# Two post-norm transformer layers on one core: attention outputs turned on VectorE, first batch projected in place, and a new deal of the steps

## The chip, the cores and the metric

One NeuronCore of a Trainium2 chip runs the whole program. The metric is the device time of one execution in microseconds (us), median over the runs shown. Everything is fp32.

## What is computed

The input x is 8 batches of 256 tokens with 128 features. Two layers follow, each an attention and a feed-forward part, each with a residual and a layer norm behind it:

```
x = layernorm(x + attn0(x))     # 16 heads of 8, softmax over 256 keys, biases
x = layernorm(x + ffn0(x))      # 128 -> 512, butterfly mixes, GELU, butterfly mixes, 512 -> 128
x = layernorm(x + attn1(x))     # low-rank q and kv, RoPE, causal, 16 heads on 4 kv heads
x = layernorm(x + ffn1(x))      # h = silu(gate) * up, hidden 384
```

The butterfly stages of ffn0 are folded on the chip into two dense matrices (`wup`, `down`) during the first steps.

## The kernel before

**Batches and steps.** The 8 batches of layer 0 are batches 0 to 7, those of layer 1 are 8 to 15, so there are 16 batches of 16 heads, 256 heads in all. Each engine has one program, and all five walk the same list of steps `STEPS` (L49), two heads a step. The step number g is the head whose exponentials are due. In a step TensorE issues the row-maximum scores of heads g+14 and g+15 (`max_scores`, L292, banks SM) and the scores to be exponentiated of heads g and g+1 (`exp_scores`, L311, banks ST), and behind them whatever is due at this g. There are three SM banks and three ST banks, so a score matmul waits until VectorE (the maximum, L668 in layer 0, L676 in layer 1) or ScalarE (the exponential, L535) has read the head three before. All other TensorE results share two G banks, handed out in order by `claim`, which waits for the last reader of the bank.

**What is due when** is an order written out by hand, the constants `AT_...` (L43 to L48): an item of batch b is due at g = 16b + offset, one of a feed-forward tile n of layer 0 (512 tokens, two batches) at 32n + offset. "Slot s" below means steps with g mod 16 = s; slots of the 32-step cycle of a tile of layer 0 are given mod 32. Per batch: projection of queries and keys (`AT_QK`, L447), values (`AT_V`, L461), two transposes of maxima (`AT_MT`, L348), products with the values for each half of the heads (`AT_PV`, L479), then the tail of the attention: ScalarE copies each half out (O, L597); at `AT_T` TensorE transposes four 128x128 blocks (L355), VectorE takes reciprocals of the row sums and multiplies (L684, L687); at `AT_ATT` TensorE transposes two blocks back (L405) and ScalarE copies (L555); at `AT_PROJ` the output projection (L415) follows; then statistics on VectorE, the norm on GpSimd (`AT_LN`, L780), transposes (L422). Layer 0 adds four up matmuls (L365), one GELU over 2048 columns on ScalarE (L602, with a table load ahead and one behind), two down groups (L389), norm and transposes. Layer 1 adds RoPE on GpSimd (`AT_ROPE`, L832 to L834), the causal mask on GpSimd (L824), three up matmuls (L376), a down group (L398).

**Queries and keys** leave the projection with one feature row per partition and are laid out by DMAs (L231, four a batch) into `QK`, where head j of a group has 32 rows of its own; row 31 of each strip takes the negated maximum (sent by a DMA from `mt`, L246) against a row of ones. `QK` has a ring of four batches.

**Start.** Batch 0 goes the same way: load, projection, copy, four DMAs. Before the first scores TensorE runs three 128x512 matmuls on a zeroed part of `QK` (L453), which GpSimd clears first (L815). Steps -14 to -2 fill the ST side with dummy matmuls (`filler`, L322). Weights for later stages are loaded by SP, one DMA a step from g = LATE = -20 on (L249).

Of the kernel before, what the change touches and what calls it, by code (L numbers as in the profile page):

```python
# [38 lines left out]
VCOL, VPAD = 32, 264  # L39
# [12 lines left out]
FIRST, FINAL = AT_QK, HEADS + 40  # L52
STEPS = range(FIRST, FINAL, 2)


def batch_at(g, offset, layers=(0, 1)):

    b, rest = divmod(g - offset, H)
    return b if rest == 0 and 0 <= b < BATCHES and b // NB in layers else None

# [14 lines left out]
def block_kernel(nc, x_nat, x_t, ones, wqk0, wv0, bqk0, bv0, wproj, bproj, u0, d0, fac_u, fac_d, bfw, bup, bcon, bdown,  # L75
# [7 lines left out]
    with ctx:  # L83
# [3 lines left out]
        def sem(name):  # L87
            return ctx.enter_context(nc.semaphore(name))

        wqk_sb = sb("wqk_sb", [P, 2, W])  # L90
# [47 lines left out]
        O = sb("O", [P, 2, 2, T])  # L138
        rec = sb("rec", [P, 4 * QT * 2, 2])
        at = sb("at", [P, QT, W])  # L140
# [15 lines left out]
        ld = {n: sem(f"ld_{n}") for n in ("x0", "x", "qk", "v", "id", "bf", "up", "bv", "bvc", "xb", "proj", "l1", "next", "rope", "gate")}  # L156
# [3 lines left out]
        bv_ps, filled = sem("bv_ps"), sem("filled")  # L160
        path_ready = [sem(f"path_ready{i}") for i in range(2)]
# [8 lines left out]
            "st_ps", "exp_done", "masked", "pv_ps", "o_ready", "t_ps", "at_ready", "att_ps", "att_ready", "proj_ps",  # L170
# [27 lines left out]
        def _(sp):  # L198
            sp.dma_start(xt[:, 0:T], x_t[:, 0:T]).then_inc(ld["x0"], 16)
            sp.dma_start(id32[:, :], ident).then_inc(ld["id"], 16)  # L200
            sp.dma_start(xt[:, T:TOK], x_t[:, T:TOK]).then_inc(ld["x"], 16)
            sp.dma_start(wv_sb[:, :], wv0).then_inc(ld["v"], 16)

            late = [(ld["bv"], wproj_sb[:, :], wproj), (ld["bv"], bproj_sb[:, :], over_partitions(bproj)),
                    (ld["up"], facs[0][:, :, :], fac_u), (ld["up"], u_sb[:, :, :], u0),
                    (ld["xb"], xb[:, :, :], x_nat),
                    (ld["bf"], bfw_sb[:, :, :, :, :], bfw), (ld["bf"], d_sb[:, :, :], d0),
                    (ld["bf"], facs[1][:, :, :], fac_d), (ld["bf"], bup_sb[:, :], bup)]
# [8 lines left out]
            for g in STEPS:  # L217
                for l in range(2):
                    if (b := batch_at(g, AT_QKIN[l], (l,))) is not None:

                        if l == 0:
                            sp.wait_ge(A["qk_out"], 2 * (b + 1))
                        else:
                            sp.wait_ge(A["rotated"], b - NB + 1)
                        if b < QK_RING:
                            sp.wait_ge(zeros_ready, b + 1)
                        else:
                            sp.wait_ge(A["st_ps"], H * (b - QK_RING + 1))

                        for j in range(2 if b == 0 else STRIPS):  # L230
                            sp.dma_start(QK[STRIP * j:STRIP * j + ROWS, b % QK_RING, :, :, :], qk[j:P:STRIPS, b % 2, :, :])\  # L231
                                .then_inc(qk_in[b % QK_RING], 16)
                        if b < QK_RING:
                            sp.dma_start(QK[MAXROW:P:STRIP, b, :, 1, :], ones).then_inc(ones_in[b], 16)
                if (b := batch_at(g - 2, AT_QK, (1,))) is not None:
# [7 lines left out]
                if (n := half_at(g - 2, AT_MT)) is not None:  # L243
                    b, t = divmod(n, 2)
                    sp.wait_ge(A["mt_ready"], n + 1)
                    sp.dma_start(QK[MAXROW:P:STRIP, b % QK_RING, 2 * t:2 * t + 2, 0, :], mt[:, n % 2, :]).then_inc(m_in[n % 4], 16)  # L246
# [11 lines left out]
        def _(pe):  # L258
# [19 lines left out]
            def max_scores(m, c):  # L278

                b, r, j = place(m)  # L280
                if c == 1:
                    if m % H == 0:
                        pe.wait_ge(qk_in[b % QK_RING], 16 * STRIPS * (b // QK_RING + 1))
                    if m >= S_RING:
                        pe.wait_ge(A["max_done"], m - S_RING + 1)
# [10 lines left out]
            def exp_scores(m, c):  # L296

                b, r, j = place(m)
                if c == 0:
# [3 lines left out]
                    if m % H == 0 and b < QK_RING:  # L303
# [3 lines left out]
                    else:  # L307
                        pe.wait_ge(filled, m + LEAD - S_RING + 1)
# [7 lines left out]
            def filler(m, c):  # L316
# [3 lines left out]
                if c == 0 and m >= S_RING - LEAD:  # L320
                    pe.wait_ge(filled, m + LEAD - S_RING + 1)
# [5 lines left out]
            def scores(g):  # L327

                for long in range(2):
# [3 lines left out]
                    for m in (g, g + 1):  # L333
                        if 0 <= m < HEADS:
                            exp_scores(m, long)
                        elif -LEAD <= m < 0:
                            filler(m, long)

            for g in STEPS:
                scores(g)  # L340

# [8 lines left out]
                if (b := batch_at(g, AT_T)) is not None:  # L350
                    bank = claim(("t", b), A["at_ready"], b + 1, g)
                    pe.wait_ge(A["o_ready"], 2 * (b + 1))
                    for q in range(QT):
# [3 lines left out]
                    ins.then_inc(A["t_ps"], 1)  # L357
# [43 lines left out]
                if (b := batch_at(g, AT_ATT)) is not None:  # L401
                    bank = claim(("att", b), A["att_ready"], b + 1, g)
                    pe.wait_ge(A["at_ready"], b + 1)
                    for q in range(QT):
                        ins = nc.tensor.transpose(bank[:, q * P:(q + 1) * P], at[:, q, :], id32[:, :])  # L405
                    ins.then_inc(A["att_ps"], 1)
# [23 lines left out]
                if (b := batch_at(g, AT_QK)) is not None:  # L430
                    x = xt[:, (b % NB) * T:(b % NB + 1) * T]
                    if layer(b) == 0:
                        bank = claim(("qk", b), A["qk_out"], 2 * (b + 1))
                        if b == 0:
                            pe.wait_ge(ld["x0"], 16)
                            pe.wait_ge(ld["qk"], 32)
                        elif b == 1:
                            pe.wait_ge(ld["x"], 16)
# [10 lines left out]
                if g == FIRST:  # L449

                    pe.wait_ge(zeros_ready, QK_RING)
                    for i in range(3):
                        nc.tensor.matmul(ST[i][:, :], QK[:, QK_RING - 1, 0, 0, 0:P],  # L453
# [555 lines left out]
```

## Time and profile before

| | |
|---|---|
| median of 3 runs | 377.0 us (376.42, 377.0, 378.9) |
| the profiled execution, its own time | 378.37 us |
| its span, first to last instruction | 376.6 us |
| around the span | 1.8 us |
| TensorE matmul busy | 341.9 us (91%) |
| VectorE busy | 238.1 us (63%) |
| ScalarE busy | 203.9 us (54%) |
| GpSimd busy | 170.8 us (45%) |
| mean granted TensorE clock | 0.970 |

Busy shares are means over stages; the span has a start (to 28 us), a layer 0 part (to about 190 us), a layer 1 part, and a tail without scores from about 355 us on. An fp32 matmul shows as two records in the profile, so "x4" is two matmuls.

### The profile page before, as it was taken

Reading aid. Unit: us, or ns where it says so; the run is one execution under the profiler, and the core shown is the slowest. Engines: PE = TensorE matmul, PEld = TensorE weight load, DVE = VectorE, ACT = ScalarE, POOL = GpSimd, SP = SyncE. Lnnn points to the kernel's source line nnn. Section 1 sums busy time; section 2 is a strip of 40 time slices with the busy share of each in tenths; the row PEclk is TensorE's granted clock in tenths of the full one; section 3 lists DMA queues with packets and bytes.
Section 4 is the critical chain, followed back from the end, with each engine's and each line's share of the span. In section 5 each row is a group of like instructions: output and inputs, shape, how many; then the busy total and the mean of one; then the engine's idle time right before and its main releaser. Section 6 shows DMA issues by size and latency. Waiting matters only on the chain.

```text
span 376.6 us, 10486 instructions
## 1 busy us (share of the span) xinstructions
PE 341.9 (91%) x3912; PEld 239.6 (64%) x3912; DVE 238.1 (63%) x907; ACT 203.9 (54%) x439; POOL 170.8 (45%) x284
## 2 busy tenths in 40 slices
PE   3989999999989999899998899799899999999872
PEld 2557666665648556575567666488677777777652
DVE  3365566577758577376764738548597878883354
ACT  2015666665694656746574545834665565656310
POOL 7036964020202502346143766616958685453621
PEclk9998999999999999899998989969999999999998
DMA  4493150101010101101111001110111111000000
GB/s 146 63 293 58 35 138 3 30 3 30 3 30 2 31 3 31 29 3 30 30 31 28 21 13 30 30 28 4 44 32 44 31 44 30 18 3 17 2 15 29
DMA packets 9219, 14.04 MB, mean 37 GB/s; under 512 B 2001, under 2 KB 4945, under 8 KB 9041
## 3 DMA queue, kind: packets, MB, share of 16 engines
q1 hardware_dynamic: 8656, 13.11, 15.1%
q8 instruction: 31, 0.51, 0.6%
q10 hardware_dynamic: 512, 0.26, 0.4%
q14 instruction: 20, 0.16, 0.2%
HBM read 5.76 MB, written 1.05 MB: 18 GB/s over the span
## 4 chain that ended last, share of the span: by engine, by line
PE 79%; POOL 6%; DVE 5%; ACT 4%; issue 3%; DMA 2%; POOLq 0%; DVEq 0%; ACTq 0%
PE SM L292 27%; PE G L479 13%; PE ST L311 6%; PE G L389 5%; PE G L376 4%; PE G L365 4%; PE G L447 3%; PE G L348 3%; PE G L355 3%; PE G L398 2%; PE G L461 2%; POOL QK L815 2%; PE G L415 2%; DMA QK<-mt 2%; PE ST L453 1%
## 5 line engine op out<-in xcount | busy, mean ns | idle before, releaser
L535 ACT ACTIVATE E<-ST 128x512 f32<-128x512 f32 (+1 forms) x256 | 125.4, 541 | 89.0 <-PE ST L311 88.8
L311 PE MATMUL ST<-QK 32*128 32x256 f32 (+1 forms) x1024 | 138.5, 380 | 9.6 <-ACT E L535 8.0
L292 PE MATMUL SM<-QK 31*128 31x256 f32 (+1 forms) x1024 | 140.2, 379 | 0.8 <-DVE mx L668 0.7
L292 PEld LDWEIGHTS SM<-QK 31*128 31x128 f32 x1024 | 93.3, 186 | 40.5 <-DVE mx L668 13.2
L668 DVE TENSOR_REDUCE mx<-SM 128x2 f32<-128x512 f32 x128 | 82.2, 685 | 56.5 <-PE SM L292 56.3
L311 PEld LDWEIGHTS ST<-QK 32*128 32x128 f32 x1024 | 91.8, 187 | 14.1 <-ACT E L535 9.9
L676 DVE CUSTOM_DVE_ANT_0 masked_s<-SM,mask_sb 128x256 f32<-128x256 f32 (+1 forms) x256 | 75.7, 351 | 36.2 <-PE SM L292 35.9
L824 POOL TENSOR_SCALAR_AFFINE_SELECT E<-E 128x512 f32<-128x512 f32 x64 | 39.1, 634 | 43.5 <-ACT E L535 43.5
L479 PE MATMUL G<-E,V 128*32 128x256 f32 x992 | 53.6, 356 | 0.0
L479 PEld LDWEIGHTS G<-E,V 128*32 128x32 f32 x992 | 28.4, 109 | 20.3 <-issue 4.6
L777 POOL TENSOR_SCALAR nm_a<-mv_a 128x2 f32<-128x2 f32 x15 | 2.9, 193 | 62.7 <-DVE mv_a L635 62.7
L376 PE MATMUL G<-xt,wf 128*128 128x256 f32 x84 | 23.0, 400 | 0.1
L597 ACT ACTIVATE O<-G 128x256 f32<-128x256 f32 x31 | 11.9, 384 | 18.0 <-PE G L479 18.0
L676 DVE DVE_READ_ACCUMULATOR2_ANT mx<- 128x1 f32 x256 | 21.2, 83 | 0.0
L777 POOL TENSOR_SCALAR nm_f<-mv_f 128x4 f32<-128x4 f32 x4 | 0.8, 195 | 43.0 <-DVE mv_f L635 43.0
L389 PEld LDWEIGHTS G<-down,hid 128*128 128x128 f32 x128 | 17.8, 220 | 1.0 <-issue 0.7
L389 PE MATMUL G<-down,hid 128*128 128x128 f32 x128 | 18.3, 303 | 0.0
L376 PEld LDWEIGHTS G<-xt,wf 128*128 128x128 f32 x84 | 15.0, 197 | 3.1 <-ACT mt L542 0.9
L365 PE MATMUL G<-xt,wup 128*128 128x512 f32 x32 | 16.8, 606 | 0.0
L542 ACT ACTIVATE mt<-G 8x256 f32<-8x256 f32 x32 | 11.4, 357 | 7.1 <-PE G L348 7.1
L447 PE MATMUL G<-xt,wqk_sb 128*128 128x256 f32 x32 | 9.9, 434 | 4.7 <-DMA bqk_sb<-bqk 4.7
L832 POOL TENSOR_TENSOR ry<-ry,ropec_sb 128x512 f32<-128x512 f32 x8 | 10.2, 1279 | 8.3 <-issue 4.9
(135 smaller groups left out, 453.8 us busy)
## 6 DMA issues: line engine op xcount, KB each, us to landing
QK<-qk SPq DMA_DIRECT2D x62, 64.0 KB
rs<-ry SPq DMA_DIRECT2D x16, 128.0 KB, 2.3
xb<-x_nat SPq DMA_DIRECT2D x1, 1024.0 KB, 8.1
out<-ln_g SPq DMA_DIRECT2D x8, 128.0 KB, 2.0
xt<-x_t SPq DMA_DIRECT2D x1, 896.0 KB, 6.7
wi<-wi_all SPq DMA_DIRECT2D x1, 576.0 KB, 4.9
QK<-mt SPq DMA_DIRECT2D x32, 8.0 KB
fac<-fac_u SPq DMA_DIRECT2D x1, 508.0 KB, 4.6
```

The lines of the kernel that those rows point to most:

```text
L292: ins = nc.tensor.matmul(SM[m % S_RING][:, cols], q, QK[rows, b % QK_RING, r, 1, keys], start=True, stop=True)
L311: ins = nc.tensor.matmul(ST[m % S_RING][:, c * T:(c + 1) * T - q0], QK[rows, b % QK_RING, r, 1, c * P:(c + 1) * P], QK[rows, b % QK_RING, ...
L365: nc.tensor.matmul(bank[:, :], wup[:, c * P:(c + 1) * P], xt[:, n * FT:(n + 1) * FT], start=True, stop=True).then_inc(F0["up_ps"], 1)
L376: ins = nc.tensor.matmul(bank[:, s * T:(s + 1) * T], wf[:, s, c * P:(c + 1) * P], xt[:, i * T:(i + 1) * T], start=True, stop=True)
L389: ins = nc.tensor.matmul(bank[:, i * W:(i + 1) * W], hid0[:, c, s * P:(s + 1) * P], down[:, c, :], start=(c == 0), stop=(c == HC - 1))
L447: ins = nc.tensor.matmul(bank[:, s * T:(s + 1) * T], w[:, s, :], x, start=True, stop=True)
L479: ins = nc.tensor.matmul(bank[VCOL * j:VCOL * (j + 1), q0:T], values, E[:, (2 * n + e) % E_RING, j, k * T:(k + 1) * T - q0], start=(e == 0 ...
L535: act.activation(E[:, a % E_RING, j, 0:n], ST[m % S_RING][:, 0:n], ACT.Exp, scale=SCALE)\
L597: act.activation(O[:, b % 2, t, :], g_bank["pv", n][:, 0:T], ACT.Copy).then_inc(A["o_ready"], 1)
L668: ins = nc.vector.tensor_reduce(mx[:, n % 2, :, i], bank[:, :].rearrange("p (q k) -> p q k", q=QT), AX.X, ALU.max, negate=True)
L676: ins = nc.vector.tensor_tensor_reduce(out=masked_s[:, m % 2, lo:hi], in0=bank[:, lo:hi], in1=mask_sb[:, T + lo - hi:T], scale=-1.0, scala ...
L824: nc.gpsimd.affine_select(out=e, in_=e, pattern=[[0, 4], [1, P]], compare_op=ALU.is_ge, fill=0.0, base=0, channel_multiplier=-1).then_inc( ...
```

## The change

1. **Attention outputs on VectorE.** The ScalarE copies O and att and both sets of TensorE transposes go. VectorE transposes each PV bank in 32x32 blocks into `turned` (one 128x256 instruction at each PV step), takes reciprocals at `AT_NORM` = 22, GpSimd multiplies (128x256), and at `AT_ATT` = 24 VectorE transposes the product into `att`. The order of the value columns is changed to match.
2. **Batch 0 in place.** `wfirst` holds, for each of the four head groups, the query and key weights already spread over the 32-row strips; four projections (at g = -44, -12, -8, -4) are copied by ScalarE straight into `QK`, with the row of ones as a bias. No layout DMAs for batch 0. The three first matmuls read a tile `idle` that VectorE clears. The filler runs for 8 heads, not 14.
3. **Loads.** Weights of later stages are issued by SP right behind x; only the rest waits for `LATE` = -2. Batch 1's four layout DMAs are issued by ScalarE.
4. **A new deal.** See the constants: odd batches' queries and keys at 16b - 44 (the step behind GELU's), even ones of layer 1 at 16b - 40, values of layer 0 at -8 (even) or -2 (odd), the third up matmul of layer 1 at 44 (was 40), the third of layer 0 at 64 (was 56), RoPE at -34 (was -28), the last norm at 56 (was 50). SP now looks for the DMA of the maxima before the layout DMAs.

```
-AT_QK, AT_QKIN, AT_ROPE = -34, (-32, -24), -28
-AT_MT, AT_V, AT_PV = (-6, 2), 0, (12, 20)
-AT_T, AT_ATT, AT_PROJ, AT_LN, AT_XT = 22, 24, 26, 28, 32
-AT_UP1, AT_DN1, AT_LN1 = (34, 38, 40), 46, 50
-AT_UP0, AT_GELU, AT_DN0, AT_LN0, AT_XT0 = (50, 54, 56, 66), 66, (70, 72), 74, 80
-BXU, BXD, TURN, JOIN, BV, XB_AT, WF_AT, LATE = (4, 6), 16, 32, 22, 0, 14, 38, -20
+AT_QK, AT_QKIN, AT_ROPE = (-34, -40, -44), -28, -34
+AT_MT, AT_V, AT_PV = (-6, 2), ((-8, -2), (0, 0)), (12, 20)
+AT_NORM, AT_ATT, AT_PROJ, AT_LN, AT_XT = 22, 24, 26, 28, 32
+AT_UP1, AT_DN1, AT_LN1 = (34, 38, 44), 46, 56
+AT_UP0, AT_GELU, AT_DN0, AT_LN0, AT_XT0 = (50, 54, 64, 66), 66, (70, 72), 74, 80
+BXU, BXD, TURN, JOIN, BV, XB_AT, WF_AT, LATE = (4, 6), 16, 32, 22, 0, 14, 38, -2
+FIRST, FINAL = AT_QK[2], HEADS + 44
+FIRST_AT, EARLY, FILL = (FIRST, -12, -8, -4), (None, -10, 2), 8
...
# TensorE
+            pe.wait_ge(idle_ready, 1)
+            for i in range(S_RING):
+                nc.tensor.matmul(ST[i][:, :], idle[:, 0:P], idle[:, :], start=True, stop=True)
...
+                for r in range(GROUPS):
+                    if g == FIRST_AT[r]:
+                        bank = claim(("first", r), first_out, 2 * (r + 1))
...
+                        for s in range(2):
+                            ins = nc.tensor.matmul(bank[:, s * T:(s + 1) * T], wfirst_sb[:, r, s, :], xt[:, 0:T], start=True, stop=True)
...
-                        for t in range(2):
-                            ins = nc.tensor.transpose(bank[:, (2 * q + t) * P:(2 * q + t + 1) * P],
-                                                      O[:, b % 2, t, q * P:(q + 1) * P], id32[:, :])
...
-                        ins = nc.tensor.transpose(bank[:, q * P:(q + 1) * P], at[:, q, :], id32[:, :])
...
# ScalarE
-                    act.activation(att[:, :], g_bank["att", b][:, 0:T], ACT.Copy).then_inc(A["att_ready"], 1)
...
-                    act.activation(O[:, b % 2, t, :], g_bank["pv", n][:, 0:T], ACT.Copy).then_inc(A["o_ready"], 1)
...
+                            act.activation(QK[:, 0, r, s, :], g_bank["first", r][:, s * T:(s + 1) * T], ACT.Identity,
+                                           bias=bfirst_sb[:, r, s:s + 1]).then_inc(first_out, 1)
...
# VectorE
+                    nc.vector.reciprocal(rec[:, :, :], found[:, :, 2 * D:2 * D + 2]).then_inc(A["rec_ready"], 1)
...
+                    nc.vector.transpose(att[:, :].rearrange("p (x t c) -> p x t c", t=2, c=2 * D), at[:, :, :, :].rearrange("p t x c -> p x t c"))\
+                        .then_inc(A["att_ready"], 1)
...
+                    nc.vector.transpose(turned[:, t, :], g_bank["pv", n][:, 0:T]).then_inc(A["turned"], 1)
...
# GpSimd
+                    nc.gpsimd.tensor_tensor(at[:, :, :, :].rearrange("p t x (e d) -> p (t x) e d", d=D),
+                                            found[:, :, 0:2 * D].rearrange("p x (e d) -> p x e d", d=D),
+                                            rec[:, :, :].unsqueeze(3).broadcast_to([P, 2 * T // BLOCK, 2, D]), ALU.mult)\
+                        .then_inc(A["at_ready"], 1)
```

## Rows read from the trace of the kernel before

**Rows 1.** Busy time by stage: PE, PEld, DVE, ACT, POOL, clock, DMA.
```profile
87.00:214.00 127.00, 120.28 (x1388) 79.37 (x1390) 83.14 (x268) 78.82 (x153) 40.62 (x68) 0.97 0.10 20
...
286.00:341.00 55.00, 54.09 (x730) 41.76 (x722) 43.76 (x247) 32.92 (x84) 35.30 (x64) 1.00 0.13 28
```

**Rows 2.** Groups by line: the second set of transposes (busy, mean ns, idle before).
```profile
L405 PE MATMUL G<-id,at 128*128 128x128 f32 x30 | 5.8, 275 | 0.2 <-DVE at L687 0.2
```

**Rows 3.** Groups by line on the other engines: busy, mean ns, idle before.
```profile
L687 DVE TENSOR_TENSOR at<-G,rec 128x256 f32<-128x256 f32 x15 | 6.4, 424 | 0.5
...
L697 DVE TENSOR_SCALAR hid<-G,bhid 128x512 f32<-128x512 f32 x16 | 12.0, 747 | 0.4 <-PE G L365 0.3
L597 ACT ACTIVATE O<-G 128x256 f32<-128x256 f32 x31 | 11.9, 384 | 18.0 <-PE G L479 18.0
...
L832 POOL TENSOR_TENSOR ry<-ry,ropec_sb 128x512 f32<-128x512 f32 x8 | 10.2, 1279 | 8.3 <-issue 4.9 <-DMA rs<-ry 3.4
...
L853 POOL TENSOR_TENSOR xb<-ln_a,bcon_sb 128x256 f32<-128x256 f32 x8 | 5.9, 735 | 0.7
```

**Rows 4.** The chain in layer 1, slots 6 to 12: start, us, what.
```profile
289.86 0.41 PE SM L292 x2
...
290.72 0.59 PE G L355 x4
291.31 0.88 PE G L376 x4
...
295.48 0.38 PE G L348 x2
...
296.31 0.41 PE SM L292 x2
```

**Rows 5.** Timeline of VectorE, 288 to 308 us: its idle times.
```profile
290.74 0.42 DVE L676 CUSTOM_DVE_ANT_0 masked_s<-SM,mask_sb 128x256 f32<-128x256 f32 x1 [0.75 <-PE SM L292]
...
299.50 0.42 DVE L676 CUSTOM_DVE_ANT_0 masked_s<-SM,mask_sb 128x256 f32<-128x256 f32 x1 [0.74 <-PE SM L292]
```

**Rows 6.** Timeline of the start, 0 to 31 us.
```profile
7.65 1.88 ACTq L577 DMA_DIRECT2D QK<-qk  x2
...
7.90 5.18 PE L453 MATMUL ST<-QK 128*128 128x512 f32 x6 [1.15 <-POOL QK L815]
...
13.97 0.48 PE L292 MATMUL SM<-QK 31*128 31x256 f32 x2
...
22.36 0.58 SPq L246 DMA_DIRECT2D QK<-mt  x1
...
28.24 0.48 PE L311 MATMUL ST<-QK 32*128 32x256 f32 x2 [1.64 <-DMA QK<-mt]
```

**Rows 7.** Timeline around the first GELU, layer 0.
```profile
101.16 1.13 PE L447 MATMUL G<-xt,wqk_sb 128*128 128x256 f32 x4
...
109.92 1.28 ACT L535 ACT_TABLE_LOAD   x1
...
111.87 0.48 PE L311 MATMUL ST<-QK 32*128 32x256 f32 x1 [1.85 <-ACT E L535]
```

**Rows 8.** The chain behind the first and the third GELU.
```profile
113.58 1.79 PE G L389 x16
...
201.35 1.04 PE G L355 x4
202.40 2.51 PE G L389 x16
...
216.37 0.89 POOL ln_a L780 x2
...
217.40 0.63 PE G L422 x2
```

**Rows 9.** The chain in the tail, 354 to 366 us.
```profile
356.90 0.39 ACT O L597
...
360.63 0.70 PE SM L415 x4
```

More of the change, by code:

```diff
@@ L59, in batch_at, with by_layer, projected_at, values_at @@
     return b if rest == 0 and 0 <= b < BATCHES and b // NB in layers else None
+def by_layer(g, offsets):
+    found = [batch_at(g, offsets[l], (l,)) for l in range(2)]
+    return found[0] if found[0] is not None else found[1]
+def projected_at(g):
+    if g in EARLY:
+        return EARLY.index(g)
+    b = batch_at(g, AT_QK[2])
+    if b is not None and len(EARLY) <= b < BATCHES - 1 and b % 2 == 1:
+        return b
+    b = by_layer(g, AT_QK)
+    return b if b is not None and b >= len(EARLY) and (b % 2 == 0 or b == BATCHES - 1) else None
+def values_at(g):
+    for l in range(2):
+        for parity in range(2):
+            b = batch_at(g, AT_V[l][parity], (l,))
+            if b is not None and b % 2 == parity:
+                return b
+    return None
+def loads_of(b):
+    return b // QK_RING + (1 if b % QK_RING else 0)
 def half_at(g, offsets):
@@ L88, in sem @@
             return ctx.enter_context(nc.semaphore(name))
+        wfirst_sb = sb("wfirst_sb", [P, GROUPS, 2, W])
+        bfirst_sb = sb("bfirst_sb", [P, GROUPS, 2])
+        idle = sb("idle", [P, 512])
         wqk_sb = sb("wqk_sb", [P, 2, W])
@@ L154, in block_kernel @@
         G = [ctx.enter_context(nc.psum_tensor(f"G{i}", [P, 512], F32)) for i in range(2)]
-        ld = {n: sem(f"ld_{n}") for n in ("x0", "x", "qk", "v", "id", "bf", "up", "bv", "bvc", "xb", "proj", "l1", "next", "rope", "gate")}
+        ld = {n: sem(f"ld_{n}") for n in ("x0", "x", "first", "groups", "qk", "v", "id", "bf", "up", "bv", "bvc", "xb", "proj", "l1", "next", "rope", "gate")}
         zeros_ready, v_clean, half_ready = sem("zeros_ready"), sem("v_clean"), sem("half_ready")
@@ L217, in _ @@
             for g in STEPS:
[L218 to L235, printed above, removed]
+                if (n := half_at(g - 2, AT_MT)) is not None:
+                    b, t = divmod(n, 2)
+                    sp.wait_ge(A["mt_ready"], n + 1)
+                    sp.dma_start(QK[MAXROW:P:STRIP, b % QK_RING, 2 * t:2 * t + 2, 0, :], mt[:, n % 2, :]).then_inc(m_in[n % 4], 16)
+                b = projected_at(g - 2)
+                if b is None or layer(b) == 1:
+                    b = batch_at(g, AT_QKIN, (1,))
+                if b is not None and b != 1:
+                    if layer(b) == 0:
+                        sp.wait_ge(A["qk_out"], 2 * b)
+                    else:
+                        sp.wait_ge(A["rotated"], b - NB + 1)
+                    if b < QK_RING:
+                        sp.wait_ge(zeros_ready, b)
+                    else:
+                        sp.wait_ge(A["st_ps"], H * (b - QK_RING + 1))
+                    for j in range(STRIPS):
+                        sp.dma_start(QK[STRIP * j:STRIP * j + ROWS, b % QK_RING, :, :, :], qk[j:P:STRIPS, b % 2, :, :])\
+                            .then_inc(qk_in[b % QK_RING], 16)
+                if (b := projected_at(g - 2)) is not None and layer(b) == 1:
                     sp.wait_ge(A["y_out"], b - NB + 1)
@@ L448, in _ @@
                     ins.then_inc(A["qk_ps"], 1)
[L449 to L453, printed above, removed]
-                                         QK[:, QK_RING - 1, 0, :, :].rearrange("p s t -> p (s t)"), start=True, stop=True)
-                if (b := batch_at(g, AT_V)) is not None:
+                if (b := values_at(g)) is not None:
                     bank = claim(("v", b), A["v_ready"], b + 1)
@@ L813, in _ @@
             nc.gpsimd.memset(half[:, :], -0.5).then_inc(half_ready, 1)
-            for i in range(QK_RING):
+            for i in range(1, QK_RING):
                 nc.gpsimd.memset(QK[:, i, :, :, :], 0.0).then_inc(zeros_ready, 1)
@@ L967, in _arrays @@
     kcol = [2 * D * (h // rep) + 2 * d, 2 * D * (vh // rep) + 2 * vd + 1]
+    wfirst, bfirst = np.zeros((P, GROUPS, 2, P), np.float32), np.zeros((P, GROUPS, 2), np.float32)
+    bfirst[MAXROW::STRIP, :, 1] = 1.0
+    for s, cols in enumerate((q, k)):
+        for i, c in enumerate(cols):
+            row, head = divmod(i, H)
+            to = STRIP * (head % STRIPS) + row
+            wfirst[:, head // STRIPS, s, to], bfirst[to, head // STRIPS, s] = wqkv[:, c], bqkv[c]
     u = np.concatenate([a["L0_ffn_W_exp"].T, a["L0_ffn_b_exp"][:, None]], 1)
```

162 lines of the change are left out of this document (85 added, 77 removed).

## The prediction

> **What bounds the kernel now.** First the busy time by stage [rows 1]: TensorE has 95% of the stretch 87 to 214 us and 98% of 286 to 341 us. So between the ends TensorE's own list of work is the time, and each item taken off it counts unless another wait comes up behind it. VectorE is next: 80% in 286 to 341 us (43.76 of 55.00). Its timeline [rows 5] shows between two idle times, 290.74 and 299.50 us, four steps without a pause. The chain there [rows 4] leaves TensorE after the matmul at 291.31 and comes back only at 295.48, through VectorE. So slots 6 to 10 of a layer 1 batch are already VectorE's, the rest TensorE's. Then the start [rows 6]: the first real scores stand at 13.97 us and the first exponential scores at 28.24 us, where TensorE waits for the DMA of the maxima, issued 22.36 us. Then GELU [rows 7]: ScalarE reloads its table at 109.92, and TensorE stands 1.85 us for an exponential. Last, behind the GELUs [rows 8]: this GELU is the third, and behind it four-block transposes took 1.04 us against 0.59 in rows 4, the sign of a TensorE clock of 1.2 GHz instead of 2.4 after a stall, and the transposes at 217.40 wait for GpSimd's norm (end at 217.26).
>
> **Removed on TensorE.** Per batch 0.59 us of four transposes [rows 4] and about 0.29 of two (5.8 us over 15 batches is 0.38 with overlap, [rows 2]; start to start it is less). 16 x 0.88 = 14.1 us is the most this can give. ScalarE loses three copies of 0.38 a batch [rows 3], which is off the path except in the tail.
>
> **Added.** VectorE gets three 128x256 block transposes a batch and loses one multiply; the reciprocal stays. The trace has no VectorE transpose. Nearest rows [rows 3]: 0.42 us for a 128x256 multiply and 0.75 us for a 128x512 pass. I take 0.42 (same element count, one pass) and keep 0.25 to 0.75 as ends, the lower since part of a short instruction overlaps its neighbour. So VectorE has 3 x 0.42 - 0.42 = +0.84 us a batch, 13.4 us in all. Two of the three stand behind a PV group, the longest item of TensorE, where VectorE idles (the 0.75 us of rows 5), at no cost. The third stands in slot 8, in VectorE's own stretch. GpSimd gets a multiply of 0.74 us [rows 3], between reciprocal (slot 6) and transpose (slot 8); a step lasts 1.6 us or more, so it is hidden.
>
> The Trainium skill (VectorE: DVE Perf Modes, section "The three transpose paths") gives 311 ns for a 128x128 bf16 transpose on VectorE, in 32x32 blocks. If 256 columns cost two of these, an estimate of 0.62 us from that page, the transpose in slot 8 would cost 0.2 more a batch, 3.2 in all, and the time would be 365.6 instead of 362.4. No row here shows a VectorE transpose; it is to be read from the run.
>
> **Slots 6 to 12, the heart.** Layer 1 before: 6.45 us from the start of slot 6 (289.86) to that of slot 12 (296.31) [rows 4]. After: slot 6 loses 0.59, slot 8 loses 0.29 and the third up matmul (0.88), which goes to slot 12. TensorE alone would need 4.7. VectorE's list is two heads (1.1 us a step), reciprocal 0.35, two up passes 0.84, transpose 0.42: slot 8's first maximum is ready 3.8 us after slot 6 starts, so slot 10 can't start before that, and slot 12 starts at 5.35. With 0.88 paid at slot 12 this is 6.2: a gain of 0.25 where slot 8 is else empty. Where it holds the projection (0.87, every second batch) the hole is filled, and the gain is 1.1. That makes 1.4 us in two batches, of 1.8 removed. In layer 0 it is the same with the values (0.6) in slot 24: 0.3 of 0.88 kept there, and 0.4 in the half without up matmuls.
>
> **The sum by stages**, against the profiled execution's own 378.37 us (span 376.6 and 1.8 around it):
> - *Start.* The layout DMAs of batch 0 and the 7 us wait for GpSimd's clears go. Warm-up from about 2 to 7.3 us (5.18, [rows 6]), projection of the first group 1.1 to 2, copy 0.85: scores at about 9.3 instead of 13.97. But then each of groups 1 to 3 is projected in the step just ahead of its first score, so TensorE waits 1.0 + 0.9 us for matmuls and ScalarE's copy, three times, and ScalarE issues batch 1's four DMAs between (1.88 us for two, so 3.3 to 3.8), ahead of group 2's copy: about 3 us of stall. Step 0 comes at about 26 us, as before (25.9). The gain is behind it: the maxima's DMA, 5.8 us then in a queue of big loads, is now issued when these have landed; 2.3 us of wait end. Batch 2's and 3's projections come into steps 2 and 4 where the values left and steps were short. I take 2.5 us; 0 to 5.
> - *Steps 0 to 66*, before the first GELU: transposes in three batches, partly VectorE's: 1.3.
> - *66 to 130*, two tile cycles of layer 0. GELU pins its exponential at 111.87 [rows 7], so the odd batch's projection (1.06 to 1.13 us) behind GELU costs nothing; after the stall 0.59 of transposes goes, but the down group's bank is read by ScalarE's copy of that projection, which ends 0.3 late: 0.3. Further on, norm on GpSimd arrives at the same time as TensorE now, so the lighter slots 8 and 14 there are eaten by that wait. From XT0 to the next GELU 1.1. So 1.4 a cycle, 2.8.
> - *130 to 194.* There GpSimd's chain decides [rows 8]. In the first tile 0.6 off the head of it and 0.4 later: 1.0. In the second the third up matmul is also gone from ahead of the down group, 0.59 + 0.9 + 0.5: 2.0. RoPE (3 x 1.28, [rows 3]) now stands ahead of the mask of heads 12 to 15 instead of behind; PV needs it 5.8 us after XT at the tightest, GpSimd needs 5.1: close, taken as 0.
> - *194 to 256*: 62/32 x 1.4 = 2.7.
> - *Tail.* ScalarE copy, transposes, up matmuls in the way, transposes, copy: from 356.90 to 360.63 is 3.73 us [rows 9]. After: 0.42 + 0.35 + 0.74 + 0.42 and four hand-overs of 0.1 = 2.4. Gain 1.3.
> - *Clock.* Behind three of the four GELUs the clock fell. In rows 8 that cost 0.45 on the transposes (1.04 against 0.59) and 0.7 on the down group (2.51 against 1.79), with scores between 1.5; three times, and the last stall held it twice as long: about 5 in all. With 1.1 us of matmuls in each stall it may not fall; against that stand new stalls in the start. I take 1.0, nearer to nothing, since the wait at XT stays.
> Sum: 2.5 + 1.3 + 2.8 + 3.0 + 2.7 + 1.3 + 1.0 = 14.6. So 363.8 for an execution like the profiled one. That one lay 1.4 above the median, so 377.0 - 14.6 = 362.4 us, a ratio of 0.961. Its own range is 359 to 367.
>
> **Rivals.**
> 1. *The clock stays up.* The silence of TensorE behind GELU shrinks by 1.1 us. For it: the down group behind the stall of rows 7 ran at full clock (1.79, [rows 8]), so not every such stall costs it. Against: the wait at XT behind it remains. All 5.0 instead of 1.0: 358.4.
> 2. *VectorE transposes are dear or its list decides more widely.* At 0.75 us each 1.0 more a batch, of which a third stands in the full stretch and some of the rest at PV: 16 x 0.4 = 6.4 less: 368.8. For it: 80% busy already; against: the rows of equal shape.
> 3. *The start gives nothing or costs.* If TensorE falls to its lower clock without the filler in steps -14 to -10 and in the 3 us stall, its seven steps take 0.5 more each and the gain of 2.5 turns into -1.5: 366.4.
> 4. *Slower than before: GpSimd becomes the pace of layer 1.* In each batch it holds masks 4 x 1.22, RoPE 3.8, norms 4, and now a multiply for which it waits behind VectorE's reciprocal with the next mask queued behind. If PV waits on that mask, each of 8 batches pays multiply, wait and RoPE's rest: 0.74 + 0.6 + 1.1 = 2.4, 19.5 in all, of which the 14.6 pays most: 377.0 - 14.6 + 19.5 = 381.9. It decides once GpSimd is past 17 us in a batch; [rows 1] give it 35.30 of 55.00 us, 64%. So it is unlikely.
> 5. *The change doesn't do what it says*: the removed work was cover for waits throughout, result within 1%: the 95% and 98% of rows 1 speak against it.
>
> **Chances.** Forecast 0.50; clock up 0.18; dear VectorE 0.13; start 0.13; GpSimd 0.03; nothing 0.03. A difference under about 1% can't be told from none here. Faster by over 1% takes the first four: 0.94; same 0.03; slower 0.03. The range takes in the clock rival to most of its size and cases 2 and 3 together: 355 to 370.
>
> **What would show it.** TensorE has no transposes but those of maxima and norms, and its busy sum falls by 12 to 15 us. VectorE shows three transposes a batch, 0.4 us each, busy up by some 13 us, with the waits of max scores on VectorE longer. First real score near 9 us, first exponential score near 26, with a stall for ScalarE's copies between. At GELU the stall on the exponential is about 1 us shorter with a projection ahead of it. Tail from last PV to output projection 2.4 us. Wrong if the VectorE transpose is far from 0.42, if step 0 comes later than 28 us, or if PV waits for the mask over 0.5 us a batch.

## Result: a quarter of the forecast

The changed kernel takes 375.3 us (median of 20 runs, 372.96 to 378.79) beside 378.9 us for the kernel before (20 runs on the same chip). The ratio is 0.991, 95% interval 0.989 to 0.993. The forecast was 0.961, or 14.6 us. The profiled execution of the changed kernel has a span of 373.5 us against 376.6 before, so 3.1 us are there. The direction was right, the size was not.

**Where it came and went.** The step number g names the same point in both kernels, so the start of the first score matmul of a step (timeline of TensorE) can be set side by side. "End" is the end of TensorE's last matmul.

| from the start of | to | before, us | changed, us | gain | forecast |
|---|---|---|---|---|---|
| span | step 8 | 36.94 | 40.72 | -3.8 | +2.5 |
| step 8 | 66 | 67.17 | 65.01 | +2.2 | +1.3 |
| 66 | 130 | 88.69 | 85.09 | +3.6 | +2.8 |
| 130 | 194 | 92.64 | 87.52 | +5.1 | +3.0 |
| 194 | 254 | 65.62 | 65.32 | +0.3 | +2.7 |
| 254 | end | 20.22 | 24.48 | -4.3 | +1.3 |
| clock | | | | in the rows above | +1.0 |
| sum | | | | +3.1 | +14.6 |

So the middle gave more than was forecast (10.9 against 7.1 and the clock's 1.0), the two ends lost 8.1 where 3.8 had been expected, and steady layer 1 gave nothing.

**The profile after.** First the page of the changed kernel: busy time and its share, and two groups, then a third from the list of groups.

```profile
span 373.5 us, 10260 instructions
...
PE 340.0 (91%) x3804; PEld 234.7 (63%) x3804; DVE 250.9 (67%) x940; ACT 189.2 (51%) x397; POOL 178.1 (48%) x299
...
L885 POOL TENSOR_TENSOR at<-turned,rec 128x256 f32<-128x256 f32 x16 | 10.1, 628 | 94.9 <-DVE rec L726 94.9
...
L805 DVE STREAM_TRANSPOSE turned<-G 128x256 f32<-128x256 f32 x31 | 13.9, 449 | 16.8 <-PE G L524 16.6
```
```profile
L731 DVE STREAM_TRANSPOSE att<-at 128x256 f32<-128x256 f32 x16 | 7.0, 437 | 0.0
```

The block transpose on VectorE takes 0.45 us out of PSUM and 0.44 us out of SBUF, beside the 0.42 that was taken from [rows 3]. VectorE's sum rose by 12.8 us, as forecast (13). TensorE's sum fell by only 1.9 us where 12 to 15 were forecast, although the transposes are gone. The granted clock explains little of that: 22.7 us of TensorE's busy time stand at the lower clock, against 19.8 before. Part of the fall was never there to be had: where records overlap the sum counts them once, and without those of L355 and L405 the sum of the kernel before is 11.0 us less, not the prediction's 14.1. Part 1 of the change alone takes 7.0 off it (334.9 us, see the experiments); where the rest went isn't settled. The clock does explain why a later version with the same 10260 instructions shows 330.6: it has only 5.9 us of busy time at the lower clock, 16.8 less, and half of that is 8.4 of the 9.4 us between the two. This is the first thing to learn here: busy time isn't work.

**The start**, against [rows 6]. TensorE, then ScalarE (start us, us, engine, line, what, idle before and its releaser; L406 projects a group of batch 0, L498 queries and keys of batch 1):

```profile
6.39 1.03 PE L406 MATMUL G<-xt,wfirst_sb 128*128 128x256 f32 x4
8.34 1.13 PE L342 MATMUL SM<-QK 31*128 31x256 f32 x10 [0.93 <-ACT QK L610]
...
13.37 2.07 PE L342 MATMUL SM<-QK 31*128 31x256 f32 x8 [0.93 <-ACT QK L610]
15.37 2.08 PE L498 MATMUL G<-xt,wqk_sb 128*128 128x256 f32 x4
...
19.40 1.23 PE L406 MATMUL G<-xt,wfirst_sb 128*128 128x256 f32 x4
...
22.47 0.48 PE L342 MATMUL SM<-QK 31*128 31x256 f32 x2 [1.39 <-ACT QK L610]
...
27.50 0.48 PE L342 MATMUL SM<-QK 31*128 31x256 f32 x2 [0.93 <-ACT QK L610]
```
```profile
18.36 3.17 ACTq L626 DMA_DIRECT2D QK<-qk  x4
21.57 0.84 ACT L610 ACTIVATE QK<-G,bfirst_sb 128x256 f32<-128x256 f32 x2 [3.25 <-PE G L406]
```

The first score stands at 8.34 instead of 13.97, 5.6 us early where 4.7 were forecast. All of it is gone by step -6 (22.47 against 19.91). Each of the three later projections stands just ahead of its first score, and ScalarE's copy is waited for each time; the four DMA issues of L626 hold the second of these copies back (projection ended 20.6, copy begins 21.57); and L498 takes 2.08 us here against 1.06 elsewhere. That last one is the clock. Busy time by stage, of the changed kernel (us, PE, PEld, DVE, ACT, POOL, then the granted clock):

```profile
12.00:20.00 8.00, 7.07 (x33) 4.19 (x32) 2.09 (x4) 1.68 (x4) 7.37 (x13) 0.57 0.07 23
20.00:30.00 10.00, 7.34 (x71) 4.97 (x73) 4.68 (x9) 2.32 (x6) 5.17 (x6) 0.99 0.40 143
30.00:38.00 8.00, 8.00 (x54) 4.99 (x48) 3.45 (x7) 3.58 (x8) 4.51 (x1) 0.58 0.00 1
```

Before, the same stretches had 1.00, 0.99 and 0.80. TensorE is at 1.2 GHz for most of 12 to 20 us and again of 30 to 38.

**Layer 1, slots 6 to 12**, against [rows 4] and [rows 5]: the chain (start, us, what) and VectorE's timeline.

```profile
282.99 0.41 PE SM L342 x2
...
283.86 1.06 PE G L435 x4
...
285.78 1.06 PE G L498 x4
...
288.54 0.41 PE SM L342 x2
...
289.41 1.06 PE G L435 x4
290.47 1.44 PE G L524 x32
```
```profile
283.06 0.45 DVE L805 STREAM_TRANSPOSE turned<-G 128x256 f32<-128x256 f32 x1
283.87 0.42 DVE L716 CUSTOM_DVE_ANT_0 masked_s<-SM,mask_sb 128x256 f32<-128x256 f32 x1 [0.36 <-PE SM L342]
...
284.99 0.35 DVE L726 RECIPROCAL rec<-turned 128x32 f32<-128x32 f32 x1
...
287.27 0.44 DVE L731 STREAM_TRANSPOSE att<-at 128x256 f32<-128x256 f32 x1
```

From slot 6 to slot 12 it is 5.55 us (forecast 5.35), VectorE having no pause in it behind 283.87, and then the third up matmul (289.41) costs 1.06 (forecast 0.88). This is the batch with a projection in slot 8 (285.78); the two behind it, without one, take 5.56, so that projection is hidden, as forecast.

**Behind the third GELU**, against [rows 8], the chain:

```profile
198.96 2.01 PE G L448 x16
...
208.66 1.26 POOL xb L924
...
212.43 0.89 POOL ln_a L834 x2
...
213.45 0.41 PE G L475 x2
```

The first down group takes 2.01 us where [rows 8] have 2.51 behind transposes of 1.04. GpSimd's norm is still what TensorE waits for, at 213.45.

**The tail**, against [rows 9], the chain:

```profile
351.75 0.45 DVE att L731
...
352.33 0.70 PE ST L468 x4
...
355.97 0.34 DVE gated L751
...
356.33 0.43 DVE hid L753
...
356.90 2.31 PE ST L457 x12
359.21 0.44 PE G L475 x2
...
360.20 2.05 PE G L435 x4
362.25 2.86 PE SM L435 x8
```

Before, the output projection (360.63) was followed by norm and transposes alone, and the transposes stood 3.79 us behind it (364.42). Now they stand 6.88 behind (359.21), since VectorE's two passes for the third up of the batch before (355.97) and its down group (356.90) are in between.

### The profile page after: what moved, and what is told of

Read it like the earlier page. It is cut to its first block, busy times and chain, and to the rows that moved or that the text cites. A ratio compares the mean times of both kernels' runs of the same rounds, so it can differ in the third digit from the quotient of the medians.

```text
span 373.5 us, 10260 instructions
## 1 busy us (share of the span) xinstructions
PE 340.0 (91%) x3804; PEld 234.7 (63%) x3804; DVE 250.9 (67%) x940; ACT 189.2 (51%) x397; POOL 178.1 (48%) x299
## 4 chain that ended last, share of the span: by engine, by line
PE 73%; POOL 9%; issue 6%; ACT 5%; DVE 5%; ACTq 1%; POOLq 0%; DVEq 0%
PE SM L342 26%; PE G L524 10%; PE ST L361 6%; PE G L435 5%; PE G L448 4%; PE G L498 4%; PE G L424 3%; PE G L457 2%; PE G L415 2%; PE G L506 2%; POOL ln_f L834 2%; ACT L580 1%; PE G L468 1%; POOL xb L924 1%; PE ST L392 1%
## 5 line engine op out<-in xcount | busy, mean ns | idle before, releaser
L342 PE MATMUL SM<-QK 31*128 31x256 f32 (+1 forms) x1024 | 146.6, 384 | 8.0 <-ACT QK L610 4.2
L342 PEld LDWEIGHTS SM<-QK 31*128 31x128 f32 x1024 | 97.7, 189 | 49.0 <-DVE mx L708 13.3
L885 POOL TENSOR_TENSOR at<-turned,rec 128x256 f32<-128x256 f32 x16 | 10.1, 628 | 94.9 <-DVE rec L726 94.9
L805 DVE STREAM_TRANSPOSE turned<-G 128x256 f32<-128x256 f32 x31 | 13.9, 449 | 16.8 <-PE G L524 16.6
L448 PE MATMUL G<-down,hid 128*128 128x128 f32 x128 | 16.3, 281 | 0.1
L435 PEld LDWEIGHTS G<-xt,wf 128*128 128x128 f32 x76 | 13.4, 196 | 4.6 <-ACT xt L599 0.9
L448 PEld LDWEIGHTS G<-down,hid 128*128 128x128 f32 x128 | 15.0, 191 | 1.9 <-issue 0.7
L751 DVE SCALAR_TENSOR_TENSOR gated<-th,G 128x256 f32<-128x256 f32 x19 | 8.0, 420 | 10.0 <-ACT th L594 9.9
L834 POOL TENSOR_SCALAR ln_a<-r_a,nm_a,rstd_a 128x128 f32<-128x128 f32 x30 | 13.2, 447 | 1.6
L415 PE MATMUL G<-id,mx 128*8 128x128 f32 x64 | 12.7, 280 | 0.0
```

The lines of the kernel that those rows point to most:

```text
L342: ins = nc.tensor.matmul(SM[m % S_RING][:, cols], q, QK[rows, b % QK_RING, r, 1, keys], start=True, stop=True)
L415: ins = nc.tensor.transpose(bank[0:8, q * P:(q + 1) * P], mx[:, n % 2, q, :], id32[:, :])
L435: ins = nc.tensor.matmul(bank[:, s * T:(s + 1) * T], wf[:, s, c * P:(c + 1) * P], xt[:, i * T:(i + 1) * T], start=True, stop=True)
L448: ins = nc.tensor.matmul(bank[:, i * W:(i + 1) * W], hid0[:, c, s * P:(s + 1) * P], down[:, c, :], start=(c == 0), stop=(c == HC - 1))
L834: ins = nc.gpsimd.tensor_scalar(N["ln"][:, parity, s, :], N["r"][:, s, :], N["nm"][:, s:s + 1], N["rstd"][:, s:s + 1], ALU.add, ALU.mult)
```

## Experiments

All ratios are to the kernel before, run on the same chip, with 95% intervals; times of steps are from the profiled executions. In each, what isn't named is as in the changed kernel.

### Third up of the last two batches earlier

```
+def up1_at(g, c):
+    b = batch_at(g, AT_UP1[c], (1,))
+    if c == SC - 1:
+        if b is not None and b >= BATCHES - 2:
+            b = None
+        if (e := batch_at(g, 40, (1,))) is not None and e >= BATCHES - 2:
+            b = e
+    return b
```

> Edit: the third up matmul of the last two batches goes back to offset 40 (step 264 for batch 14, ahead of the last output projection); all others stay at 44. Theory A (in the tail that up matmul sits behind the last output projection, so its two VectorE passes queue behind batch 15's residual, statistics and norm, and the down group of batch 14 delays the transposes of batch 15; the stall then lowers TensorE's clock): last projection to its transposes falls from 6.67 us to about 3.8, the last up matmuls to the last down group from 6.4 to about 4.3; 4 to 5 us in all, ratio to before about 0.979. Rival B (the tail is long because block transposes and the GpSimd multiply are a slower way than TensorE's): under 1 us, ratio 0.989 or more.

Ratio 0.976 (0.970 to 0.981), span 370.1. All steps up to 254 start within about 0.1 us of the changed kernel's; TensorE ends at 364.77 instead of 368.14. The chain of its tail:

```profile
352.44 0.70 PE ST L479 x4
...
356.23 0.42 PE G L486 x2
...
358.82 2.92 PE SM L446 x8
```

The transposes are back at 3.79 us behind the projection, exactly as before. So 3.5 of the 5.6 us by which the tail missed its term are this one constant, 44 instead of 40, at two places. The expected 4 to 5 us fall short by what the clock still takes: a stretch at the lower clock remains in the tail (2.92 us for eight matmul records, 1.74 in the version below with the third up at 40 throughout).

### Filler for 14 heads instead of 8

```
-FIRST_AT, EARLY, FILL = (FIRST, -12, -8, -4), (None, -10, 2), 8
+FIRST_AT, EARLY, FILL = (FIRST, -12, -8, -4), (None, -10, 2), 14
```

> Edit: dummy score matmuls in all seven steps -14 to -2, as before the change (FILL = 14). Theory A (the clock fell at 13.1 us because TensorE had only the real scores to do in steps -14 to -10): the clock holds to the wait for ScalarE's DMA issues, batch 1's projection takes 1.1 instead of 2.0 us, step 0 comes 2 to 3 us earlier; ratio about 0.983. Rival B (the stalls between the groups lower it, filler or not): step 0 within 1 us of 28.5, ratio 0.989 to 0.993.

Ratio 0.980 (0.973 to 0.986), span 369.2. The granted clock is 1.00 in 12 to 20 and in 30 to 38 us. Step 0 stands at 26.42 (2.1 earlier), step 8 at 35.77 (4.9 earlier). So the start's loss of 3.8 at step 8 is more than explained by the clock: without its falls the start gives +1.2. How much of the 4.9 us is the filler's own is less sure: the first stretch at the lower clock (from 12.8 us) stands in all five profiled kernels with this start (the changed one and the four edits of it that leave the projections and the filler of the start alone) and in none of the five with more filler or earlier projections, but the second (from 29.9 us) is missing in two of the former too.

### First projections early

```
-FIRST_AT, EARLY, FILL = (FIRST, -12, -8, -4), (None, -10, 2), 8
+FIRST_AT, EARLY, FILL = (FIRST, FIRST + 2, -12, -8), (None, -10, 2), 8
```

> Edit: the four in-place projections of batch 0 move one group earlier: group 1 right behind group 0 (step -42), group 2 at -12, group 3 at -8. The first real score comes about 1.1 us later. Theory A (each group is projected just ahead of its first score, so TensorE waits for matmul and copy, and group 2's copy stands behind four DMA issues of ScalarE): the steps -12, -8 and -4 of 4.3, 5.1 and 3.7 us become 2 to 3 us, step 0 comes 4 to 5 us earlier (about 24) and the clock stays up with it; ratio 0.977 to 0.980. Rival B (the clock alone makes the start long): 1 us or less.

Ratio 0.966 (0.962 to 0.971), span 365.5. Each group is projected one step or more ahead of its first score. Step 0 stands at 22.50 (6.0 earlier), step 8 at 31.47 (9.2 earlier), more than the 4 to 5 us expected at step 0. The timeline of its start and its stages:

```profile
6.10 1.89 PE L406 MATMUL G<-xt,wfirst_sb 128*128 128x256 f32 x8
8.06 1.13 PE L342 MATMUL SM<-QK 31*128 31x256 f32 x10
...
13.15 1.13 PE L498 MATMUL G<-xt,wqk_sb 128*128 128x256 f32 x4
```
```profile
12.00:20.00 8.00, 6.64 (x63) 4.56 (x66) 3.88 (x7) 3.07 (x8) 7.37 (x13) 1.00 0.21 59
20.00:30.00 10.00, 9.66 (x100) 6.95 (x96) 6.99 (x12) 4.92 (x12) 9.32 (x7) 1.00 0.38 126
30.00:38.00 8.00, 7.92 (x102) 5.35 (x98) 5.16 (x8) 5.39 (x12) 0.25 (x1) 1.00 0.57 83
```

L498 takes 1.13 instead of 2.08 us, and the clock stays up with no filler added: without the waits for copies there is no fall. Beside the filler experiment (4.9 at step 8) the other 4.3 us are the waits themselves.

### Batch 1's DMAs issued by SyncE

```
-                if b is not None and b != 1:
+                if b is not None:
...
-                        if b == 1:
-                            act.wait_ge(A["qk_out"], 2)
-                            act.wait_ge(zeros_ready, 1)
-                            for j in range(STRIPS):
-                                act.dma_start(QK[STRIP * j:STRIP * j + ROWS, 1, :, :, :], qk[j:P:STRIPS, 1, :, :]).then_inc(qk_in[1], 16)
```

> Edit: batch 1's four layout DMAs are issued by SP, not by ScalarE. Theory A (the 3.17 us in which ScalarE issues them are in the chain, since group 2's copy stands behind them): step -8 falls from 5.1 to about 2.7 us, step 0 comes 2.3 us earlier; ratio about 0.985. Rival B (TensorE would wait for the same copies anyway, for the projections are late): under 0.7 us, ratio 0.989.

Ratio 0.981 (0.976 to 0.987), span 370.3. Step 0 comes only 0.4 us earlier (28.10): ScalarE's copy begins at 21.19 instead of 21.57, because now the projection ahead of it, at the lower clock, ends last. Yet step 8 stands at 37.46, 3.3 earlier. The stages say why: the first fall is there still, the second is gone.

```profile
12.00:20.00 8.00, 7.07 (x33) 4.19 (x32) 2.10 (x5) 1.68 (x4) 7.37 (x13) 0.59 0.06 21
...
30.00:38.00 8.00, 8.00 (x80) 5.86 (x79) 5.06 (x9) 6.38 (x15) 4.52 (x1) 1.00 0.15 31
```

So the path named by theory A is worth 0.4 us, as in rival B, and the rest goes with the second fall. That the issues caused this fall isn't shown: it is missing as well in the kernel with the third up at 40 in all batches, whose start is the changed kernel's. Which gap in TensorE's work between 20 and 30 us decides over it wasn't taken apart.

### Part 1 alone

The kernel before with the outputs turned on VectorE, and nothing else of the change (start, loads and deal stay):

```
+                    nc.vector.transpose(turned[:, t, :], g_bank["pv", n][:, 0:T]).then_inc(A["turned"], 1)
...
-                    act.activation(O[:, b % 2, t, :], g_bank["pv", n][:, 0:T], ACT.Copy).then_inc(A["o_ready"], 1)
```

> Edit: the kernel before with part 1 of the change alone (block transposes on VectorE, multiply on GpSimd, value columns reordered); start, loads and the deal of the steps as before. TensorE loses 0.88 us a batch. Theory A (VectorE's full stretch in slots 6 to 10 keeps about half of it, the tail gains 1.3 us, the clock behind GELU falls as before): 7 to 9 us, ratio 0.976 to 0.982. Rival B (VectorE is the pace wherever the transposes went): under 3 us, ratio 0.993 or more. Rival C (all of it arrives): 14 us, ratio 0.963.

Ratio 0.983 (0.979 to 0.988), span 369.8. TensorE ends 6.8 us earlier than in the kernel before (a little under the 7 to 9 expected), so this part alone is worth more than twice the whole change. The lead at steps 66, 130, 194 and 254 is 1.3, 1.9, 4.3 and 5.9, and the tail gives 0.9. Behind the first GELU the clock fell, where it hadn't in the kernel before; why there isn't settled. Its chain:

```profile
112.53 3.71 PE G L381 x16
```

against 1.79 for the same down group in [rows 8].

### Third up at 40 in all batches

```
-AT_UP1, AT_DN1, AT_LN1 = (34, 38, 44), 46, 56
+AT_UP1, AT_DN1, AT_LN1 = (34, 38, 40), 46, 56
```

> Edit: the changed kernel with the third up matmul of layer 1 at offset 40 for all eight batches, as before the change. Theory A (in the step of the value products it costs TensorE 1.07 us and frees VectorE's stretch for less than that, so the move to 44 is a loss of some 0.2 us a batch without a projection in slot 8 and near nothing with one; in the tail it costs 3.5 us): steps 194 to 254 take 0 to 1.5 us less than 65.3 us, tail as in the run with the two last batches moved; ratio 0.976 to 0.980. Rival B (the move relieves VectorE as predicted): steps 194 to 254 take 2 us more, and the sum is 1 to 2 us faster than the changed kernel only for the tail.

Ratio 0.973 (0.969 to 0.977), span 364.6. Steps 194 to 254 take 63.71 us instead of 65.32 (1.6 less), the tail 19.32 instead of 24.48 (5.2 less). Step 8 also came 2.6 us earlier (38.09), of which 2.1 were left at step 194: steps 2 to 8 ran at full clock. The edit doesn't touch them, so this part isn't counted to it, and it may be why the ratio is better than the 0.976 to 0.980 expected. Of the 5.2 us of the tail 3.5 are those of the first experiment; the other 1.7 are the clock, which is full up to TensorE's end here. The lengths of the steps of slots 6, 8, 10 and 12, worked out from the starts of the score matmuls in the four profiled executions:

| | slot 6 | 8 | 10 | 12 | sum |
|---|---|---|---|---|---|
| before | 2.32 | 2.14 | 2.00 | 2.30 | 8.76 |
| changed | 1.93 | 0.77 | 2.86 | 3.36 | 8.92 |
| third up at 40 | 1.93 | 1.93 | 2.40 | 2.30 | 8.56 |
| part 1 alone | 1.93 | 1.93 | 2.40 | 2.30 | 8.56 |

(A batch without a projection in these slots; with one, slots 6 to 14 sum to 12.03 before, 11.31 changed, 11.07 with the third up at 40.) Of the 1.16 us that slot 8 saved by losing the third up, 0.46 came back in slot 10, where VectorE is behind, and slot 12 paid 1.06 for it.

### Odd queries and keys not behind GELU

```
-    b = batch_at(g, AT_QK[2])
-    if b is not None and len(EARLY) <= b < BATCHES - 1 and b % 2 == 1:
-        return b
     b = by_layer(g, AT_QK)
-    return b if b is not None and b >= len(EARLY) and (b % 2 == 0 or b == BATCHES - 1) else None
+    return b if b is not None and b >= len(EARLY) else None
```

> Edit: the changed kernel with the odd batches' queries and keys no longer behind GELU: layer 0 at 16b - 34 (slot 14), layer 1 at 16b - 40 (slot 8), so the stall of TensorE behind GELU is as long as before the change. Theory A (the projection in the stall keeps TensorE's clock at 2.4 GHz there): the clock falls again behind two or three of the four GELUs, steps 98 to 104, 130 to 136 and 162 to 168 take 1.2 to 2.5 us more each, 4 to 6 us in all, ratio about 1.003. Rival B (the clock is a matter of phase, the gain was only the hidden projection): no low clock there, 1 to 2 us, ratio 0.994 to 0.997.

Ratio 1.010 (1.006 to 1.013), span 379.7: slower than before. Up to step 8 it is within 1 us of the changed kernel; at step 194 it is 6.0 behind, at 254 7.7. The loss is larger than theory A put it. The steps that hold a GELU's end (70, 102, 134, 166):

| | 70 | 102 | 134 | 166 |
|---|---|---|---|---|
| before | 5.99 | 7.59 | 7.27 | 10.27 |
| changed | 4.71 | 4.54 | 4.25 | 5.93 |
| odd ones moved back | 5.60 | 7.20 | 6.76 | 9.86 |

These four are 10.0 us longer than in the changed kernel; the projections that no longer stand in the step ahead of each give 1.06 back four times, 4.2 in all, which leaves 5.8. Its chain behind the third GELU, and the stage 150 to 255 us of it, of the changed kernel and of the kernel before:

```profile
200.47 3.45 PE G L445 x16
```
```profile
150.00:255.00 105.00, 94.58 (x1048) 66.35 (x1048) 66.71 (x316) 56.30 (x105) 48.77 (x76) 0.92 0.11 25
```
```profile
150.00:255.00 105.00, 96.70 (x1136) 66.99 (x1138) 72.65 (x346) 59.32 (x112) 52.78 (x84) 0.98 0.13 28
```
```profile
150.00:255.00 105.00, 95.52 (x1072) 67.80 (x1072) 63.73 (x308) 61.05 (x119) 49.76 (x74) 0.92 0.13 25
```

The wait for GELU and its table load are the same (1.9 and 1.28 us in both chains), only what TensorE does ahead of it differs. With a projection there, the granted clock of the stage is 0.98; without it 0.92, as before. The stretches at the lower clock begin at 156.3, 200.7, 217.8 and 245.1 us here, at 156.0, 200.4, 217.4 and 244.8 in the kernel before, and in the changed kernel there is one, from 214.2. So it is this move that keeps the clock.

### The gains together

Three kernels, of the edits above: early first projections with the third up of the last two batches at 40; early first projections with all at 40; and the latter with SyncE issuing batch 1's DMAs.

```
+FIRST_AT, EARLY, FILL = (FIRST, FIRST + 2, -12, -8), (None, -10, 2), 8
...
+AT_UP1, AT_DN1, AT_LN1 = (34, 38, 40), 46, 56
...
+                if b is not None:
```

> Edit: the changed kernel with both cures, the four in-place projections one group earlier and the third up matmul of the last two batches at offset 40. If the two losses are separate (start, tail), their gains add: 9 to 9.5 us of start and 3.5 of tail off the changed kernel, some 362.5 us, ratio 0.957 to 0.960. If the tail's gain was the clock's phase, about 366 us, ratio 0.966.

Ratio 0.963 (0.960 to 0.967), span 361.5; step 8 at 31.30, end 356.12, so 12.0 us off the changed kernel where 12.5 to 13 were expected. The start gives 9.4. The tail takes 19.32 us, as in the kernel with all third ups at 40 (19.32), so what that one's tail had over the first experiment's is the clock and not the other batches' third ups. Steps 194 to 254 take 66.92 instead of 65.32, with a short stretch at the lower clock in them (from 332.7 us).

> The changed kernel with both of the edits that gained alone: the first projections early (FIRST_AT = FIRST, FIRST + 2, -12, -8) and the third up of every batch at step 40. If the gains add: the start of step 8 stands near 31.4 us (9.3 before the changed kernel's), steps 194 to 254 take about 63.7 us instead of 65.3, the tail from step 254 to TensorE's end about 19.3 instead of 24.5, so that TensorE ends near 368.2 - 9.3 - 7.5 = 351 us (ratio near 0.95). Rival: what the start gains is given back behind the GELUs, where batches come to the same slots with less slack, or the short clock falls take it; then the end is near 356, as with the third up moved for the last two batches only.

Ratio 0.957 (0.952 to 0.962), span 359.0; step 8 at 31.35, step 194 at 270.58, step 254 at 334.30, end 353.62. Steps 194 to 254 took 63.71 and the tail 19.32, both to 0.1 of what adding asks for. The end is 353.6 instead of 351. Steps 8 to 194 took 1.6 us more than in the changed kernel, with a granted clock of 0.97 instead of 1.00 in 87 to 214 us; the rest is the expectation's own sum, whose parts (9.3, 1.6 and 5.2) make 352. Its page:

```profile
span 359.0 us, 10260 instructions
...
PE 330.6 (92%) x3804; PEld 230.1 (64%) x3804; DVE 250.4 (70%) x940; ACT 189.1 (53%) x397; POOL 178.2 (50%) x299
```

> As the kernel with the early first projections and the third up at 40, and batch 1's DMAs issued by SyncE instead of ScalarE. With the projections' copies already early, ScalarE's issues (4 x 3.17 us in the changed kernel's start) may cost nothing: then step 8 stands within 0.3 us of that kernel's. Rival: they still hold the copies of the third and fourth group, and step 0 comes 0.5 to 1 us earlier without them.

Ratio 0.952 (0.948 to 0.956), span 358.4, 360.4 us median. Step 8 stands at 31.22 against 31.35, and step 0 at 22.24 against 22.37, though its first score came 1.2 us later (9.09 against 7.94), the cause of which wasn't followed up. So from the first score to step 0 it is 1.3 us shorter, but TensorE ends only 0.6 earlier (353.03), and the intervals of the two ratios overlap: a gain of this edit isn't shown. It is the fastest of the study by its median, 18 us below the kernel before on the same chip (378.7).

## Why the prediction was wrong

**Start: +2.5 forecast, -3.8 measured. The step that failed.** The mechanics were put right: first score "at about 9.3" (8.34), a wait of about 1.9 us at each of three projections (2.1, 3.1 and 2.1 from projection to score), ScalarE's issues "3.3 to 3.8" (3.17). But the step that turned them into "step 0 comes at about 26 us" took TensorE at full clock; it came at 28.49, past the 28 us that the prediction gave as a sign of being wrong, and the gain behind it, put at 2.3 us for the DMA of the maxima, was eaten by a second fall. The third rival named this, with a chance of 0.13 and -1.5 us for one stretch of seven steps. There were two stretches, and by the filler experiment they cost 4.9 us. That the filler shrank from 14 heads to 8 in the same change stood in the diff; its price was never set against the term. 9.2 us more were to be had from the same design by projecting one step earlier.

**Tail: +1.3 forecast, -4.3 measured. The step that failed.** From the last products to the projection the step was near: the projection stands 8.67 us behind step 254 instead of 9.57, a gain of 0.9 where 1.3 were put down, with the transpose 0.45 instead of 0.42. What failed is what the term left out: the third up was counted in the steps, with 0.88 each, and not in the last two batches, where its matmuls, VectorE's gate behind them and the down group stand between the last projection and its norm. 3.5 us of it are shown by the first experiment. The other 1.7 go with a stretch at the lower clock in the tail: where it is missing, with all third ups at 40 or with the last two and the early start, the tail takes 19.32 us, 0.9 less than before.

**Steady layer 1: +2.7 forecast, +0.3 measured. Mis-sized, twice, and once miscounted.** 5.55 instead of 5.35 us from slot 6 to 12, and 1.06 instead of 0.88 for the third up in the step of the products: 6.61 against the 6.45 of [rows 4], so a batch without a projection loses 0.16 where 0.25 was to be gained. With a projection it gains 0.71 instead of 1.1. And of the batches that pass these slots between 194 and 254 only one has a projection there, where every second one was assumed. VectorE's list in slots 8 to 10 was named as the limit, rightly; that a matmul taken out of slot 8 gives less than itself while VectorE decides (0.70 us up to slot 12), and costs all of itself there (1.06), follows from the working ("paid at slot 12"), but this move was never priced by itself.

**GELU stages: +5.8 forecast without the clock, +8.7 measured; clock +1.0. The clock was undersized, the rest was not.** With the odd projections moved back, at a clock as before, steps 66 to 194 take 179.0 us: 2.3 less than before. The other 6.4 belong to that one move, which hides four projections and keeps the clock; the two aren't fully separated, but the 5.8 us left in its four steps are near the 5 that the prediction priced. The first rival, that the clock stays up behind GELU, came true in the middle (0.98 against 0.92), and the seventh experiment ties it to the projection ahead of the stall. It had a chance of 0.18 and 4 us more. It held, but against it stood the falls in the start and in the tail, which this rival didn't price.

**VectorE's transposes: right.** Taken 0.42, measured 0.45 and 0.44. The second rival falls: part 1 alone gained 6.8 us, and it has all of VectorE's added work. The estimate of 0.62 us that was worked out from the Trainium skill (VectorE: DVE Perf Modes, "The three transpose paths") is refuted by the same row, 449 ns; for 128x256 fp32 the cost here is near that of an elementwise pass of the same size.

**GpSimd: right.** Its multiply takes 0.63 us where 0.74 was taken; GpSimd is busy 35.06 of 55 us in 286 to 341, as before (35.30). The fourth rival falls. The fifth put the result within 1% of before, and there it is (0.991), but not by its mechanism: the removed work wasn't cover throughout, since its removal alone gives 6.8 us.

The error had one root: every gain was taken from the steady pattern, where rows were plenty, while the start and the tail got one term each. The parts of a change that move work in order show their price at the ends, where nothing else is there to cover it.

## What to carry to other kernels

Walk a new order of work through the first and the last batch, queue by queue, with the same care as the steady pattern: here the ends lost 8 of the 11 us that the middle gained, and an edit of a constant at each place won them back. Where an item is moved off a step, ask which engine decides that step; if it is another one, the move saves less than the item there (0.70 us) and pays for it in full where it lands (1.06 us). And when filler or waits change, price the granted clock as a term of its own: put real matmuls ahead of a stall that can't be avoided, and project a step early rather than just in time.

## What was not expected of the hardware

- With one projection (about 1.06 us of matmuls) moved ahead of a wait of unchanged length, the mean granted clock of 150 to 255 us is 0.98 instead of 0.92, and the four steps at GELU are 10.0 us shorter together, 5.8 of them beyond the projections' own time.
- TensorE's busy time went from 340.0 to 330.6 us with the same 10260 instructions in another order; 8.4 of the 9.4 us are the lower clock's.
- A fall of the clock can be there in one profiled execution and missing in another with the same work in that place: moving the third up in layer 1 changed nothing in the start, yet there one of two stretches at the lower clock was missing (step 8 at 38.09 instead of 40.72), as it was with four DMA issues taken from ScalarE. Differences of 2 to 3 us between two profiled executions are therefore no verdict by themselves; those of the same steps at the same clock are.
